# A transformer kernel on one core: filler matmuls in the middle stage, the experts' first operands made early, the last divisions spread out

## The reference, cut to what matters

```python
xn = layernorm(x); s = L0_attn(xn)        # 16 heads, differential, causal, group norm, Wo
g  = silu(L0_ffn(xn)); x = x + s * g      # mxfp4-rounded 256 x 256 linear
xn = layernorm(x); s = L1_attn(xn)        # 16 heads of 16, causal
# L1_ffn: a mixture of experts over all tokens
h1 = einsum('td,eid->tei', xt, W1); h3 = einsum('td,eid->tei', xt, W3)
y  = einsum('tei,edi->td', silu(h1) * h3 * combine[:, :, None], W2)   # 16 experts of 176
z  = silu(xt @ Ws1.T) * (xt @ Ws3.T) @ Ws2.T
g  = silu(y + z); x = x + s * g
```

## Time and profile before

| | before |
|---|---|
| median of 3 runs | 819.36 us |
| profiled execution | 819.07 us |
| its span in the profile | 817.3 us |
| PE busy | 759.5 us, 93% of the span |
| DVE, ACT, POOL busy | 535.5, 429.3, 423.0 us |
| matmuls recorded | 3750 |
| mean granted TensorE clock | 0.974 of full |

### The profile page before, as it was taken

One profiled execution on the slowest core, in us unless ns is written; L12 is line 12 of the kernel. 1 busy time (PEld: TensorE's weight loads), 2 busy tenths in 40 slices (PEclk: granted clock), 3 DMA queues, 4 the chain that ended last, 5 costly groups with the idle time before them and its releaser, 6 DMA issues. The chain is left out here.

```text
span 817.3 us, 12994 instructions
## 1 busy us (share of the span) xinstructions
PE 759.5 (93%) x3750; PEld 370.9 (45%) x3750; DVE 535.5 (66%) x1358; ACT 429.3 (53%) x922; POOL 423.0 (52%) x755
## 2 busy tenths in 40 slices
PE   5878999999999999997998898999799999999995
PEld 3342222222232222223863232332277888888883
DVE  3878877777777777704755886875076555455556
ACT  2523566666666666662143365776644554455552
POOL 2752566664234324430223132335389997799994
PEclk9999999999999999995899999999999999999997
DMA  6493630110011002001046247443432221122221
GB/s 197 154 298 108 152 91 15 36 51 18 15 45 41 18 20 64 15 22 53 1 148 165 79 94 216 150 137 111 144 98 64 64 64 49 55 65 62 67 68 55
DMA packets 56978, 68.84 MB, mean 84 GB/s; under 512 B 13792, under 2 KB 35713, under 8 KB 56914
## 3 DMA queue, kind: packets, MB, share of 16 engines
q1 hardware_dynamic: 56840, 68.10, 29.1%
q10 hardware_dynamic: 80, 0.07, 0.0%
HBM read 46.37 MB, written 15.44 MB: 76 GB/s over the span
## 5 line engine op out<-in xcount | busy, mean ns | idle before, releaser
L816 ACT ACTIVATE top<-ps 128x512 f32<-128x512 f32 (+3 forms) x384 | 170.5, 491 | 125.6 <-PE ps L744 125.6
L744 PE MATMUL ps<-mid 99*128 99x512 bf16 (+3 forms) x576 | 181.7, 331 | 5.7 <-ACT mid L816 3.1
L858 DVE CUSTOM_DVE_ANT_0 ps<-ps,keep 128x512 f32<-128x512 f32 (+3 forms) x320 | 162.0, 530 | 26.8 <-PE ps L720 26.4
L720 PE MATMUL ps<-mid 96*128 96x512 bf16 (+3 forms) x512 | 167.5, 339 | 6.8 <-PEq L249 2.7
L764 PE MATMUL ps<-top,mid 128*33 128x512 f32 (+3 forms) x768 | 160.9, 498 | 0.0
L1638 PE MATMUL ps<-xp,wp 128*128 128x512 f32 (+1 forms) x600 | 147.2, 394 | 5.5 <-ACT wp L1688 2.9
L744 PEld LDWEIGHTS ps<-mid 99*128 99x128 bf16 x576 | 53.4, 97 | 173.5 <-ACT top L816 103.2
L1638 PEld LDWEIGHTS ps<-xp,wp 128*128 128x128 f32 (+1 forms) x600 | 112.6, 189 | 32.1 <-ACT xp L1690 3.4
L953 POOL TENSOR_SCALAR_AFFINE_SELECT top<-top 128x128 f32<-128x128 f32 x256 | 71.2, 292 | 105.2 <-ACT top L816 103.1
L816 ACT ACTIVATE mid<-ps 128x512 f32<-128x512 f32 (+1 forms) x192 | 82.3, 494 | 57.3 <-PE ps L744 33.3
L862 DVE TENSOR_REDUCE top<-ps 128x1 f32<-128x512 f32 x128 | 88.3, 690 | 33.0 <-PE ps L720 32.5
(11 more groups left out here) (219 smaller groups left out, 880.9 us busy)
## 6 DMA issues: line engine op xcount, KB each, us to landing
mid<-part_scratch SPq DMA_DIRECT2D x9, 1152.0 KB, 8.8
part_scratch<-top SPq DMA_DIRECT2D x18, 384.0 KB, 2.9
cw_s<-combine_rows SPq DMA_DIRECT2D x48, 128.0 KB, 3.0
part_scratch<-top SPq DMA_DIRECT2D x18, 256.0 KB, 3.0
top<-in_w SPq DMA_DIRECT2D x6, 634.0 KB, 5.1
mid<-part_scratch SPq DMA_DIRECT2D x9, 384.0 KB, 4.2
top<-in_w SPq DMA_DIRECT2D x4, 640.0 KB, 7.3
top<-in_w SPq DMA_DIRECT2D x4, 633.0 KB, 5.1
```

The costliest lines, as they stand in the source:

```text
L720: nc.tensor.matmul(ps[:, s_bank(turn), 0:w], queries(pair, m)[0:PARTS, i * P:(i + 1) * P], keys(pair, m)[0:PARTS, c * 512:c * 512 + w], st ...
L744: nc.tensor.matmul(ps[:, ST_BANK + n % AHEAD, 0:w], keys(pair, m)[0:STACK, j * P:(j + 1) * P], queries(pair, m)[0:STACK, q0:q0 + w], start ...
L816: nc.scalar.activation(pr[:, n % RING, 0:w], ps[:, ST_BANK + n % AHEAD, 0:w], ACT.Exp, scale=0.25).then_inc(p_ready, 1)
L858: ins = nc.vector.tensor_tensor_reduce(bank, bank, msk[:, 512 - w:512], -1.0 if low else 1.0, 3e38 if low else -3e38, ALU.add, ALU.min if ...
```

## The change

It has five parts.

1. **The middle, PE.** 33 more `keep_busy` matmuls: 4 ahead of the first `repeat_rows`, 8 ahead of the wait for the mxfp4 copies, 5 ahead of the second `repeat_rows`, 7 ahead of the first `total`, 9 behind the second one. `heads` becomes 128 rows (rows 8 to 127 are zero), so `repeat_rows` multiplies over 128 rows and not 8; POOL clears `heads` first.
2. **The middle, order.** The split parts have eight buffers in place of five, ACT's first high part stands among its xT copies, all eight units are projected before the values, and the router's four steps become six.
3. **The end of attention 1.** DVE makes, after its last maximum, both halves of `xp` (`split_x`) and the high and low parts of w13 and w2 of units 0 and 1 (`split_weights`); between them it takes the copy of half 0 of the last pair (L826 before) from ACT. The last small DMA of w2 goes two `outputs` earlier. The copy of half 1 (`last_evac`) and the inverses of half 0 move past the joint into the experts' block.
4. **The experts' start.** SP: `combine_weights(1)` ahead of `last_outputs`, and both `last_inverses` ahead of `combine_weights(3)`. DVE: inversions after units 0 and 1; the scaling, the sum of halves and the second scaling after units 3, 4 and 5.
5. **Each expert unit.** The low part of w2 is made by DVE after `g`, no longer by POOL ahead of the low part of `g`.

The core of the diff:

```diff
@@ attention @@
+            def last_evac(act):
+
+                act.wait_ge(outs[1], PER[1] * (N - 1))
+                nc.scalar.copy(osb_odd[:, :], ps[:, 7, :]).then_inc(o_evac, 1)
...
-            def last_scaled(eng):
-                scale(eng, LASTF, 0)
-                scale(eng, LASTF, 1)
+            def last_scaled(eng, step):
+                if step == 1:
+                    sum_halves(eng, LASTF)
+                else:
+                    scale(eng, LASTF, step // 2)
...
-                            if k == 13:
-                                evac(pair, 0)
+                            if k == 13 and (first or pair < N - 1):
+                                evac(nc.scalar.copy, act, pair, 0)
...
-                        evac(N - 1, 1)
+                        if first:
+                            evac(nc.scalar.copy, act, N - 1, 1)
...
-                        inverted(dve, LASTF, 0)
+                        if first:
+                            inverted(dve, LASTF, 0)
+                        else:
+                            split_x(dve, p_ready)
+                            evac(nc.vector.tensor_copy, dve, N - 1, 0)
+                            split_weights(dve, p_ready)
...
+        def split_x(dve, p_ready):
+
+            dve.wait_ge(p_ready, 4 * PAIR)
+            for c in range(NC):
+                of = slice(c * 512, (c + 1) * 512)
+                nc.vector.tensor_copy(xp[:, 0, :, of], xT[:, :, of]).then_inc(xh_ok, 1)
+                dve.wait_ge(xh_ok, c + 1)
+                nc.vector.tensor_tensor(xp[:, 1, :, of], xT[:, :, of], xp[:, 0, :, of].bitcast(F32), ALU.subtract)
+
+        def split_weights(dve, p_ready):
+
+            dve.wait_ge(p_ready, 7 * PAIR)
+            dve.wait_ge(ld_m, 16 * 16)
+            for i in range(2):
...
@@ middle @@
             def _(pe):
+                for _ in range(4):
+                    env["keep_busy"](3)
                 pe.wait_ge(bip_ok, 3)
...
+                for _ in range(8):
+                    env["keep_busy"](3)
                 pe.wait_ge(q_ev, 3)
...
                     if t == 1:
+                        for _ in range(5):
+                            env["keep_busy"](0)
                         env["repeat_rows"](pe, 1, heads, (2, 3)).then_inc(tot, 1)
+                    if t == 6:
+                        for _ in range(7):
+                            env["keep_busy"](0)
                     if t >= 6:
                         total(t - 6)
+                for _ in range(9):
+                    env["keep_busy"](0)
...
-                for u in range(2, EARLY):
+                for u in range(2, len(UN)):
                     project(u)
                 for t in range(NT):
                     values(t)
-                for u in range(EARLY, len(UN)):
-                    project(u)
...
@@ experts @@
                 combine_weights(0)
+                combine_weights(1)
                 env["last_outputs"](sp)
-                combine_weights(1)
...
                 combine_weights(2)
-                env["last_inverses"](sp)
+                env["last_inverses"](sp, 0)
+                env["last_inverses"](sp, 1)
...
+                    if c == 0 and first:
+                        pe.wait_ge(env["o_evac1"], 16)
...
+                    if not (isinstance(n, int) and n < 2):
+                        dve.wait_ge(w2h_ok, n + 1)
+                        nc.vector.tensor_tensor(w2p[0:r, b, 1, :],
...
-                    if i == 1:
-                        env["last_inverted"](dve)
-                    if i == 3:
-                        env["last_scaled"](dve)
...
+                    if i < 2:
+                        env["last_inverted"](dve, i)
+                    if i >= 3:
+                        env["last_scaled"](dve, i - 3)
```

More of the change, by code:

```diff
@@ L534, in inverted, with sum_halves @@
                 nc.vector.reciprocal(cd[:, c, 0, :], cd[:, c, 0, :]).then_inc(inv, 1)
+            def sum_halves(eng, f):
+                to = o1[:, f, columns(1)]
+                eng.wait_ge(outs[1], PER[1] * 4 * (f + 1))
+                eng.tensor_tensor(to, to, second(f), ALU.add).then_inc(num_sum, 1)
             def scale(eng, f, c):
@@ L574, in repeat_rows @@
                 for m, bank in enumerate(banks):
-                    last = nc.tensor.matmul(ps[:, bank, :], heads[:, m, :], repeated(c)[0][0:8, :], start=True, stop=True)
+                    last = nc.tensor.matmul(ps[:, bank, :], heads[:, m, :], repeated(c)[0][:, :], start=True, stop=True)
                 return last
@@ L807, in _, with evac @@
                             value_step(done)
+                    def evac(copy, eng, pair, c):
+                        eng.wait_ge(multiplied, PAIR * pair + (8 if c == 0 else PAIR))
+                        if pair > 0:
+                            eng.wait_ge(outs[c], PER[c] * pair)
+                        rows = P if first or c == 1 else 64
+                        to = osb_odd if c == 1 else osb
+                        copy(to[0:rows, :], ps[0:rows, ACC + c, :]).then_inc(o_evac, 1)
                     @block.scalar
@@ L984, in _ @@
                             if h in (1, 2) and f > 0 and k == 8:
+                                if not first and h == 2:
+                                    sum_halves(pool, f - 1)
                                 scale(pool, f - 1, h - 1)
@@ L1032, in _ @@
                                 weights(pair)
-                        if not first:
-                            sp.dma_start(w2s[0:NI - (GI - 1) * P, GI - 1, :], w2[(GI - 1) * P:NI, :]).then_inc(ld_m, 16)
                         if first:
                             inverse_rows(sp, 0)
-                        else:
-                            inverses(sp, LASTF, 0)
                         sp.wait_ge(landed, 32 * (N + 1))
@@ L1249, in _ @@
                                      ACT.Exp, scale=-1.0).then_inc(exp_ok, 1)
-                for u in range(EARLY):
-                    split(u)
-                act.wait_ge(r1_ok, EARLY)
-                nc.scalar.copy(spl[:, (EARLY - 1) % SPL, 1, :], r1[:, (EARLY - 1) % 2, :]).then_inc(mid_ok, 1)
+                for u in range(2, len(UN) + 1):
+                    if u < len(UN):
+                        high(u)
+                    middle_part(u - 1)
                 act.wait_ge(v_clr, 1)
@@ L1539, in sweep @@
             for c in range(NC):
-                for i in range(4):
+                for i in range(6):
                     step(c, i, i)
-                with eng_fori(2, 11) as g2:
+                with eng_fori(3, 11) as g2:
                     for u in range(2):
```

176 lines of the change are left out of this document (75 added, 101 removed).

## The result

| | before | changed |
|---|---|---|
| median of 6 runs | 819.63 us (818.25 to 822.77) | 814.45 us (813.00 to 815.76) |
| profiled execution, its span | 819.07, 817.3 us | 814.48, 812.7 us |
| mean granted TensorE clock | 0.974 | 0.986 |

The ratio is 0.9931, with a 95% interval of 0.9912 to 0.995: faster, by 5.2 us, where 10.6 were forecast and the range began at 6.8 less. The middle, the joint and the first three `hidden` went nearly as the prediction said. Then a wait took half of it back.

The account below looks back on a forecast made before the run. PE bounds the expert units, so gains come only at the middle and the joint with the first units: 819.07 - 5.8 - 2.4 - 2.6 + 0.2 = 808.5, median 808.8 us; eight in ten 806.3 to 812.6.

Parts of the forecast that it names:

- the joint: Between attention 1's last value matmul and the first `hidden`: PE starts at 585.0 instead of 587.44, 2.4 us saved.
- the first three `hidden`: Experts' start: the clock holds after the shorter idle, one 0.4 us wait for `g` remains; 2.6 us saved.
- Stall 2.2 us (0 to 3.2 by the two landings): Sixth `hidden` waits for `g`, whose `cw` of unit 3 comes behind two round trips on SP: 2.2 us.
- Middle so far: 3.5 + 2.4: Middle at full clock with fillers: Wo starts 3.5 us sooner and takes 2.4 us less; 5.8 us taken.
- (b): Middle: the clock falls again ahead of Wo, the 2.4 us saved there go, 811.2 us; 20%.
- (e): Middle: fillers don't lift the clock, which falls near 368; Wo starts about 7 us later, 821.6 us; 3%.
- (d): Experts' start: the stall at unit 5 does not come because the landings are short, 806.6 us; 6%.
- (f): Joint: weights land late, DVE's list ends after PE's and holds it 1 to 2 us, about 810.3 us; 1%.
- Cost and gain: 0: Middle's new order: new PE waits balance the one that goes, net 0, up to 0.8 us off either way.
- I let the two cancel: End of attention 1: ACT's lost copy, worth 0.4 us, against POOL's masks running beside DVE work; net 0.
- (c): End of attention 1: POOL's masks slow down beside DVE, up to 2.6 us, 811.4 us; 14%.
- After that DVE has ... another 0.5 us: Units behind the stall: DVE needs 3.4 to 4.6 us a unit against PE's 4.08, costing another 0.5 us.

Follow-up runs that it names:

- the best version: The opened version with `cw` of unit 2 ahead of wo1 and bo, and attention 1's last six query/key writes ahead of pair 2's row DMAs: 804.52 us.
- the opened version: Changed kernel with SP fetching `cw` of unit 3 ahead of both inverses and a `cw` fetch between each write and its read-back: 807.18 us, ratio 0.9849.

## Why the prediction was wrong, step by step

**The step that failed** is "Stall 2.2 us (0 to 3.2 by the two landings)". The mechanism was the one it names: `cw` of unit 3 behind two blocking round trips. Its size was off, in three terms. SP reached the first write 10.2 us behind PE's start, not 9.1, since wo1, bo and `cw(2)` took 2.9 us and not 1.8. The two round trips took 8.3 us, not 6.1: each write landed in 3.45 us, where I had taken 2.2 and 2.5 against the 2.84 that the earlier trace rows showed, on the strength of a shorter landing elsewhere. That is 3.3 us on top of the 2.2, and since the units ahead ran 0.4 us behind the forecast too, it made a wait of 5.1 us. The third term was left out, without a reason: within that wait, at 602.9, the clock fell, and the next 12 matmuls and more ran at 1.2 GHz, 2.8 us more. The earlier trace rows had shown just that behind the wait of 2.93 us at the old joint. So the stalls cost +5.6 and not +0.2, and 814.5 - 5.4 would be 809.1, beside the forecast of 808.8. That it comes so near is in part luck: in these two executions attention 1 gave 1.8 us that no step had, and what stands ahead of the middle took 2.0 us longer. The same list of SP made a smaller stall in two other kernels: 4.51 us of wait and 2.2 behind it with the copy on ACT, 4.19 and 1.65 without fillers. So the size has a spread of over 1 us that the sum would have needed too. Opening the round trips gave back 7.3 us, moving one `cw` 5.4, one round trip less 4.1 (6.7, 5.2 and 4.6 by the ratios): three undoings of one cause, and in each the wait that was left was within 0.5 us of the expected one.

The Trainium skill (DMA: Bandwidth & Descriptors, Latency and other measured facts) has the memory's access time as the main part of a DMA's fixed cost, longer under load. The runs agree in direction: 1.47 us for the write ahead of the joint, 3.35 and 3.45 us behind sixteen other DMAs; the 1.44 us of the kernel with the fillers alone came after a pause, the 2.86 of the kernel before too. That the memory and not the queue makes the difference, no run here shows.

**"Middle so far: 3.5 + 2.4"**: Wo began 3.2 us sooner (20.4 against 23.6 us behind the last value matmul) and took 2.86 less: 6.1, and 6.1 with the fillers alone and the clock held. Right. Rivals (b), a fall ahead of Wo, and (e), fillers that don't lift the clock, didn't come; nor did (d), short landings, and (f), a joint held by late weights. Part 1 alone gives 4 us, after the 1.7 that it lost behind DVE's late work; the rest of the change without it nothing, after the stalls.

**"Cost and gain: 0"** for the new order: it costs 0.9 us, a little over the 0.8 that I allowed. In return it has no wait of 1.64 us at which the clock can fall; that fall cost the fillers-only kernel 1.5 us of the middle (68.45 against 66.95). It came in one of the three profiled executions that have this wait (the kernel before is the third).

**The end of attention 1, "I let the two cancel"**: the last pair took 18.28 us against 18.41 (from its row DMAs to its last value matmul). The copy gave 0.45, the splits cost 0.3. Right, by one execution of each kernel. (c), slow masks, is true of the masks (566 against 292 ns), but cost 0.3 us and not 2.6, since PE waits for few of them (among these nine for one, 0.6 us). The Trainium skill (SBUF — State Buffer, SBUF: two separate sides) says of a VectorE instruction with two SBUF inputs and a GpSimd one that reads SBUF that whichever starts first has the shared ports for its whole length, and the other is blocked. The trace agrees: the longest of these nine masks took 1305 ns (563.86 to 565.16), and the subtraction that began just ahead of it 1.22 us (563.78 to 565.00). "Every piece that moves to DVE" was too much said: the copy (L828) has one input, and that in PSUM, and no mask was there at its time (572.33 to 573.01).

**Attention 1 otherwise** shrank by 1.7 us, which no step had. PE's wait for the second gather went from 2.47 to 1.52 us, since six writes took SP 4.05 us instead of 4.89, and the waits for row maxima behind it from 1.30 and 0.42 to 0.88 and 0.16 us. Those writes took 4.05 or 4.06 us in the changed kernel, in both kernels with the fillers alone, with the copy on ACT, and in all three variants of SP's list, but 4.60 us in the changed kernel without fillers, where PE waited 1.86 us. So most of the gain goes with the fillers. By what way, and why the writes took 4.89 before, stays open.

**The joint** gave 2.5 us (2.4 forecast), **the first three `hidden`** 2.2 (2.6 forecast; the 11.0 us in the last paragraph of the prediction are its own 11.2). Right.

**"After that DVE has ... another 0.5 us"** fell: with SP's list mended, the units run at 4.08 us from the second `down` on (596.40, 600.48 in the best version), with DVE's new work in place. Of all terms one made the sum fail.

## What to carry to other kernels

A write that the same queue must wait for before it reads back is a lock on everything behind it: price it with the longest landing that the trace shows near that place, not the shortest, and put other transfers between write and read. Even that would have been short here: twice the 2.84 us of the earlier trace rows against 2.2 and 2.5 adds 1.0 us, and 2.2 were missing. A gain that moves PE's start forward moves every deadline behind it, while a transfer chain that starts at the same joint does not get shorter: lay out that chain from the new start. And a PE wait can have a second price, the clock behind it: 2.08 us of wait cost about that, 5.10 cost 7.9 (5.1 + 2.8). Between them 2.42 us cost 1.7 more, 4.19 cost 1.65 and 4.51 cost 2.2 more, and a wait of 1.64 us kept the clock twice and lost it once. So a wait below 2.1 us is no guarantee, and a sum should carry both outcomes.

## What the runs showed of the hardware that was not expected

The granted clock also falls inside attention 1, in some executions and not in others: in the stretch from 25 to 35 us behind its first matmul it was 0.83 in six of the ten profiled executions, and 1.00 in the other four. The windows of the opened version and of the changed kernel, which have the same code there:

```profile
459.60:469.60 10.00, 9.55 (x53) 2.64 (x52) 8.15 (x23) 4.06 (x10) 3.11 (x12) 0.83 0.04 10
```

```profile
460.56:470.56 10.00, 9.09 (x60) 3.09 (x60) 8.48 (x24) 4.96 (x12) 3.23 (x13) 1.00 0.04 10
```

Attention 1 took 144.8 us in the first and 143.9 in the second. PE's waits from 14 us behind the first matmul up to the fall are the same in both, so what decides it is not to be seen there. The four executions without the fall are the three with the old order of the middle and one of the seven with the new order. That may be chance; that the new order has a part in it is not ruled out, and it would then cost more than its 0.9 us. With the 365.7 to 369.1 us up to the end of attention 0, that is 1 to 3 us of a single execution that no edit here is shown to explain. A stage time, laid from the stage's own start, is free of what came before it, though not of a fall inside it; a single span is free of neither.
